# Moving the second layer's inverse roots and the last block's running sums to later ticks of a hand-laid plan

## The reference: what is computed

```python
# linear attention: phi(k) v and phi(k) are summed up along the sequence
kv_cum = jnp.cumsum(k[..., :, None] * v[..., None, :], axis=2)
k_cum = jnp.cumsum(k, axis=2)
num = jnp.einsum('bhsd,bhsde->bhse', q, kv_cum)
den = jnp.einsum('bhsd,bhsd->bhs', q, k_cum)
out = num / (den[..., None] + EPS)
...
# local attention, two layers: q and k of each head are divided by their norms
q = l2norm(q) * qs
k = l2norm(k) * ksc
q, k = rotary_xpos(q, k)
o = local_attention(q, k, v)
```

## Time and profile before

| | us |
|---|---|
| median of 3 runs | 2001.98 (2001.87 to 2004.03) |
| the profiled execution, its own time | 2009.89 |
| span of the profiled execution | 2008.1 |
| PE busy in the span | 1741.9 (87%) |
| DVE busy | 1256.6 (63%) |
| ACT busy | 1191.0 (59%) |
| POOL busy | 851.9 (42%) |

### The profile page before, as it was taken

The page is one execution under the profiler, slowest core; times in us unless marked ns, Lnnn a source line. Parts: engine busy times, 40 slices in busy tenths (PEclk is TensorE's granted clock), DMA queues, the critical chain, the costliest instruction groups (busy, mean ns, idle before and its releaser), DMA issues.

```text
span 2008.1 us, 38006 instructions
## 1 busy us (share of the span) xinstructions
PE 1741.9 (87%) x12538; PEld 1123.2 (56%) x12538; DVE 1256.6 (63%) x4105; ACT 1191.0 (59%) x3559; POOL 851.9 (42%) x985
## 2 busy tenths in 40 slices
PE   6699989998989888998999898988899798785776
PEld 5378754654566546664566456654566455463454
DVE  5244547566675567666766667666766665857764
ACT  3554547566756675657666575666665665453643
POOL 3622226533535343532554353533353255534640
PEclk9999999999989999999999999999999897897978
DMA  8256500000000000000000000000000000000000
GB/s 245 71 180 211 176 16 4 9 1 1 7 1 17 1 7 1 17 1 1 7 1 17 1 7 1 17 1 6 1 7 6 1 7 1 1 7 1 1 1 11
DMA packets 50012, 53.78 MB, mean 27 GB/s; under 512 B 6546, under 2 KB 42396, under 8 KB 49820
## 3 DMA queue, kind: packets, MB, share of 16 engines
q0 software_dynamic: 7808, 27.79, 4.3%
q1 hardware_dynamic: 42012, 23.56, 4.1%
HBM read 41.90 MB, written 9.44 MB: 26 GB/s over the span
## 4 chain that ended last, share of the span: by engine, by line
PE 46%; DVE 20%; ACT 8%; issue 7%; POOL 1%; DVEq 0%; ACTq 0%; POOLq 0%
PE ps L610 5%; PE ps L672 5%; PE ps L756 3%; DVE p L1081 3%; PE ps L589 3%; PE ps L569 3%; DVE big L1264 3%; PE ps L630 3%; PE ps L579 3%; DVE ss L1260 2%; PE ps L807 2%; PE ps L798 2%; PE ps L644 2%; PE ps L654 2%; PE ps L800 2%
## 5 line engine op out<-in xcount | busy, mean ns | idle before, releaser
L1378 POOL COPY rdx<-rden 128x256 f32<-128x256 f32 x256 | 99.6, 418 | 624.4 <-DVE rden L1098 620.0
L1081 DVE CUSTOM_DVE_ANT_0 p<-ps,mask 128x128 f32<-128x128 f32 (+1 forms) x512 | 152.2, 353 | 197.9 <-PE ps L602 176.0
L1081 DVE CUSTOM_DVE_ANT_0 p<-ps,mask,rr 128x128 f32<-128x128 f32 x512 | 148.8, 347 | 168.9 <-PE ps L598 168.8
L610 PE MATMUL ps<-ident,p 128*128 128x128 f32 x1280 | 219.4, 293 | 37.4 <-ACT p L899 30.0
L899 ACT ACTIVATE p<-p,nmax 128x128 f32<-128x128 f32 (+1 forms) x512 | 226.3, 442 | 0.0
L756 PE MATMUL ps<-wqkv,hT 128*128 128x512 f32 x384 | 196.4, 618 | 31.1 <-ACT big L978 25.9
L913 ACT ACTIVATE pt<-ps 128x384 f32<-128x384 f32 (+1 forms) x256 | 111.6, 436 | 180.7 <-PE ps L610 171.5
L898 ACT ACTIVATE p<-p,nmax 128x128 f32<-128x128 f32 x512 | 200.2, 391 | 22.1 <-DVE nmax L1081 21.4
L610 PEld LDWEIGHTS ps<-ident,p 128*128 128x128 f32 x1280 | 140.7, 145 | 116.8 <-issue 101.6
L579 PE MATMUL ps<-ident,big 128*128 128x128 f32 x512 | 86.2, 308 | 80.1 <-DVE big L1269 35.5
L1092 DVE COPY pt<-ps 128x384 f32<-128x384 f32 (+1 forms) x256 | 124.5, 486 | 49.0 <-PE ps L610 45.9
(11 more groups left out here) (260 smaller groups left out, 4060.7 us busy)
## 6 DMA issues: line engine op xcount, KB each, us to landing
slots_in<-xn SPq DMA_DIRECT2D x1, 2560.0 KB, 12.9
v<-slots_in SPq DMA_DIRECT2D x20, 128.0 KB
slots_out<-v SPq DMA_DIRECT2D x20, 128.0 KB
big<-in_x SPq DMA_DIRECT2D x4, 512.0 KB, 5.8
x<-in_x SPq DMA_DIRECT2D x8, 256.0 KB, 3.7
out_x<-x SPq DMA_DIRECT2D x8, 256.0 KB, 2.3
wqkv<-in_wqkv SPq DMA_DIRECT2D x2, 768.0 KB
xn<-in_x SPq DMA_DIRECT2D x6, 256.0 KB, 3.2
```

The source lines that it names most:

```text
L610: last = nc.tensor.transpose(bank[:, j * P:(j + 1) * P], c.p[:, u % 4, j * P:(j + 1) * P], c.ident[:, :])
L1081: last = V.tensor_tensor_reduce(out=c.p[:, u % 4, a:b], in0=bank[:, a:b], in1=mask, scale=scale, scalar=3e38, op0=ALU.add, op1=ALU.min, ac ...
```

## The change

`rr` of layer 1 of blocks 0 to 5 moves one tick later, into the tick of `kn`, right ahead of it. For block 7 the linear attention from `kv` on is counted from the first step of its layer 1 (T+36) instead of from T+27, the eight parts go one to a tick, and the three segments behind them stand closer: `kv` in T+35, T+36 and T+39, `cum` in T+37 to T+44, each `sum` a tick behind, `o1` in T+47, `oT` in T+48, `s1` in T+49. No instruction is added or taken away.

```diff
-        self.put(at + TILES + (l == 0 and 0 < b < LAST), "rr", b, l)
+        self.put(at + TILES + (0 < b < LAST if l == 0 else b < LAST - 1), "rr", b, l)
         self.put(at + TILES + 1, "kn", b, l)
...
-            l0 = self.first[(1, b, 0, 0)] + (17 if b == LAST else 0)
+            l0 = self.first[(1, b, int(b == LAST), 0)]
             for t in range(2):
                 self.put(l0 - 1 + t, "kv", b, t)
-            for n, at in enumerate((1, 2, 5, 6, 9, 10, 11, 12)):
+            for n, at in enumerate(range(1, 9) if b == LAST else (1, 2, 5, 6, 9, 10, 11, 12)):
                 self.put(l0 + at, "cum", b, n // LPARTS, n % LPARTS)
                 self.put(l0 + at + 1, "sum", b, n // LPARTS, n % LPARTS)
                 if n == 2:
                     for t in range(2, TILES):
                         self.put(l0 + at, "kv", b, t)
-            self.put(l0 + 15, "o1", b)
-            self.put(l0 + 17, "oT", b)
-            self.put(l0 + 18, "s1", b)
+            self.put(l0 + (11 if b == LAST else 15), "o1", b)
+            self.put(l0 + (12 if b == LAST else 17), "oT", b)
+            self.put(l0 + (13 if b == LAST else 18), "s1", b)
```

## The result

| | us |
|---|---|
| before, median of 4 runs | 2003.01 (2001.87 to 2005.68) |
| after, median of 4 runs | 2031.9 (2023.62 to 2032.56) |
| ratio | 1.0133, 95% interval 1.0104 to 1.0161 |
| span of the profiled execution, before / after | 2008.1 / 2030.4 |

The forecast was 2018.1 us, 16 us slower, with a range up to 2028. The sign was right, the size was not: 27 us were lost by the ratio, 29 by the medians.

What follows compares the result with a forecast made beforehand. It took PE and VectorE handing work to each other inside a tick as the bound, neither alone. Terms 12.3 + 3.4 - 6.3 - 2 - 2.3 + 7 + 2 + 0 + 2 gave +16.1 us, so 2018.1 us; range 2001 to 2028.

Steps and rivals of the forecast that it cites:

- Late keys: Layer 1 of blocks 0 to 5: `rr` ahead of `kn` delays PE's key transposes, 2.05 us a place, 12.3 us lost.
- The clock: Behind the late keys: longer PE idle halves its clock at two of five places, 1.7 us each, 3.4 us lost.
- The third rival: The clock falls at all places and in the tail, with the layernorm root at 10: 2027 to 2030 us, chance 0.09.
- (a): Block 6's `rr`: the first `kv` burst leaves, so VectorE's roots no longer wait for GpSimd; 6.3 us gained.
- (b): T+28 to T+32: two `sum`s and two `cum`s leave ticks that VectorE sets; 2 us gained.
- (c): Block 7's `rr` and `kn`: 9.4 us gained, 7.0 lost as the first burst meets `kn`; net gain 2.3 us.
- (d): Block 6's `ln2n`: the second burst at T+39 holds up VectorE's layernorm root, PE waits; 7 us lost.
- (e): T+40 to T+44: one part a tick adds `cum`'s matmul and bank wait where PE sets the pace; 2 us lost.
- (f): T+44 and T+45: `oT` and `s1` leave, the last `sum` stands before the last `scaled`; taken as 0 us.
- (g): Tail: the chain of `oT`, copy, `s1` and bias makes VectorE reach the root later; 2 us lost.
- bursts miss: Both `kv` bursts run when VectorE has no two-input work: 2000.6 to 2004 us, lower end 1998; chance 0.15.
- The late keys are taken up: PE work behind the keys at the six places absorbs the delay: sum 0.4 us, 2002.4 us; chance 0.08.

Runs made afterwards that it cites:

- part 1: Kernel before with only `rr` of layer 1 of blocks 0 to 5 one tick later, block 7 as before: ratio 1.0112, 22 us slower.
- part 2: Kernel before with only block 7's linear attention moved to its second layer, all `rr` as before: ratio 1.0036, 7 us slower.
- e4_warm: part 1 plus 24 identity transposes on PE ahead of its wait for the normed keys at the six places: 1.0055 against before, 11 us slower.
- e2_lin: The run of part 2 by itself, against the kernel before: ratio 1.0036, 7 us slower.
- e3_kv: Kernel before with all four `kv` outer products of block 7 (both GpSimd bursts) moved to T+16: ratio 0.9939, 12 us faster.
- e6_half: Kernel before with the later `rr` at only three of six places (blocks 0 to 2), block 7 as before: ratio 1.0041, 8 us slower.
- e7_lin_kv: part 2 with both of block 7's `kv` bursts moved to T+16: ratio 0.9979 against before, 4 us faster.
- e9_kv01: part 2 with only the first `kv` burst (tiles 0 and 1) moved to T+16, the second at T+39: ratio 1.0000 against before.
- e10_tail: e3_kv with block 7's `o1`, `oT` and `s1` at T+47, T+48 and T+49: ratio 0.9931 against before, 14 us faster.
- e8_both: e3_kv plus 12 identity transposes on PE ahead of the keys' wait at the six places: ratio 0.9907 against before, 19 us faster.

## Why the prediction was right about the sign and short by 11 us

Point by point, by its own steps; the sum was +16.1, and the runs gave +27 for the whole (by its ratio), +22 for part 1 and +7 for part 2, where the terms had +15.7 and +0.4. So each part came out 6 to 7 us dearer than its terms.

- **Late keys, 12.3 us:** right in mechanism, 10.9 us in the trace, 11 us by e4_warm. `masked` started as soon as its logits were there, and `expand` met `rr` and not `kn` (2.50 us again).
- **The clock, 3.4 us: the step that failed.** The prediction took two of five places at 1.7 us. The runs show the half clock behind the late keys at all six, and 11 us for it (4 to 19 by the intervals). Two things were too low: the number of places, and their length, which was taken as 3.4 us and was 3.2 to 6.5. The third rival had this mechanism, at a chance of 0.09. In the profiles with part 1 PE was idle for 3.0 to 5.3 us in front of the keys, and the clock was at the half behind them at 15 places of 15; at the places without it (in before, e2_lin, e3_kv, e6_half, e7_lin_kv, e9_kv01, e10_tail) the idle time was 0.5 to 2.9 us and the clock full at 36 of 39. All three exceptions are at block 5, and in two of them (before, e3_kv) the clock had fallen before that idle time began. The prediction worked out the new idle time rightly (3.3 us and more) and then took a share of the places, because it had found idle of that length at both levels. That does hold elsewhere: the keys of block 6's layer 0 come after 1.8 us of idle and stood at the half in all twelve traces. The idle time alone doesn't tell the clock; these runs show what it did at these six places.
- **(a) 6.3 us at block 6's root:** right. The way from `rot` to the end of `kn` went from 13.7 to 7.3 us.
- **(b) and (c), 2 and 2.3 us to block 7's `kn`:** right together; no run parts (b) from (c). 88.0 to 78.2 us, less the 6.4 of (a), is 3.4 us against 4.3. The mechanism of (c), one whole GpSimd instruction for each of three L1364, is in the row of 9.13 us.
- **(d) 7 us at block 6's layernorm root:** right, 7.5 us; 5.6 for the burst, 1.9 for `cum` (e7_lin_kv, e9_kv01).
- **(e) 2 us for the parts on PE's way and (f) 0 us for the end: mis-sized together.** The way from the root to the last `wo` grew by 7.8 us (5.2 to 6.9 in the other kernels with the parts there). Of this, 2.4 us are PE's idle time ahead of `wo`, since `scaled` waited behind the last `sum`, and 2.7 us are `wo` at the half clock; the 2.7 us that are left are the parts and what the clock cost further ahead, less the 1.6 us that `oT` and `s1` gave back by e10_tail. By these numbers (f) is 3.5 us where it stood at 0, and (e) some 4 us in this kernel (an estimate) where it stood at 2. That the longer idle time made `wo`'s clock fall isn't shown: it was below the full level (0.55 to 0.60) in all four kernels with 4.1 us of idle there, but also in e10_tail (0.69) with 1.6.
- **(g) 2 us in the tail:** right, 1.6 us, also with nothing else of part 2 there (e10_tail).
- **The rival "bursts miss"** fell: both met VectorE within 1 us of the place foreseen. As a version made on purpose (e7_lin_kv, e3_kv) it is the better kernel. "The late keys are taken up" fell: e4_warm keeps 11 us of them.

On the meeting of VectorE and GpSimd, the Trainium skill (SBUF — State Buffer, section "SBUF: two separate sides") says that the loser of the shared port pair is blocked for the other's whole instruction. The trace agrees: L299 on four elements took 2.46 us and ended with L1477.

What stays open: how the 11 us of clock would come out in a tighter measurement than 4 to 19, what made `wo`'s clock fall at the end, and whether e8_both's 19 us are more than e3_kv's 12.

## What to carry to other kernels

A small chain that stands in a stretch where its engine waits for another is free only there: before moving it, look at what ends the idle time, and put it where the engine waits anyway. Price idle PE twice, once for the wait and once for the clock of what follows, and take the clock's price from places like the one you change: here about as much again as the wait. A long GpSimd instruction costs VectorE a whole wait per instruction of a dependent chain, so put it beside reductions, PSUM reads or nothing, never beside roots; here moving two bursts of 7 us to ticks where VectorE did such work was worth 12 us.

## What the runs showed of the hardware

- The granted clock behind the keys of the six places: full at 36 of 39 where PE had been idle for 0.5 to 2.9 us, half at 15 of 15 where it had been for 3.0 to 5.3 us, and then for 3.2 to 6.5 us. At another place (block 6's layer 0) it was at the half behind 1.8 us of idle in all twelve traces. With 24 transposes of the identity in the idle time it was full at all six, and the kernel 11 us faster.
- VectorE's 128x4 instructions, 0.16 to 0.17 us by themselves, took 1.48, 2.14 and 2.46 us beside GpSimd's 128x1152 ones; the TENSOR_REDUCE of 128x288 (L1239) stayed at 1.2 to 1.3 us for two beside GpSimd. Copies out of PSUM weren't held up: all 256 of L1092 took 0.41 to 0.56 us in the kernel before, with GpSimd busy beside some of them.
